# Two conditioned transformer layers on one core: the preparation put in another order, with most modulation blocks inside the slots of the first samples

## What is computed

```python
mod = swish(c) @ w_mod + b_mod
sh_msa, sc_msa, g_msa, sh_mlp, sc_mlp, g_mlp = split(mod, 6)
xn = _ln(x) * (1 + sc_msa) + sh_msa
q, k, v = heads(xn @ w_qkv + b_qkv)
q, k = _ln(q, g_q), _ln(k, g_k)          # layer 0 only
o = softmax(q @ k.T * HD ** -0.5) @ v
x = x + g_msa * (o @ w_proj + b_proj)
xn2 = _ln(x) * (1 + sc_mlp) + sh_mlp
x = x + g_mlp * (gelu(xn2 @ w1 + b1) @ w2 + b2)
```

## Time and profile before

| what | value |
|---|---|
| median of three runs | 2647.27 us (2644.73 to 2651.49) |
| the profiled execution | 2644.36 us, with a span of 2642.6 us |
| TensorE (PE) busy | 2495.9 us, 94% |
| VectorE (DVE), ScalarE (ACT), GpSimd (POOL) busy | 69%, 60%, 26% |
| mean granted clock of TensorE | 0.982 of full speed |
| first MLP product starts (slot 49 of sample 0) | 231.64 us |

### The profile page before, as it was taken

One profiled execution on the slowest core, in us unless ns is written; L12 is line 12 of the kernel. 1 busy time (PEld: TensorE's weight loads), 2 busy tenths in 40 slices (PEclk: granted clock), 3 DMA queues, 4 the chain that ended last, 5 costly groups with the idle time before them and its releaser, 6 DMA issues.

```text
span 2642.6 us, 59200 instructions
## 1 busy us (share of the span) xinstructions
PE 2495.9 (94%) x22440; PEld 2107.7 (80%) x22440; DVE 1831.6 (69%) x3700; ACT 1572.5 (60%) x2861; POOL 677.2 (26%) x937
## 2 busy tenths in 40 slices
PE   4678999999999999999999999999999999999998
PEld 2456888888888888888887788888888888888878
DVE  4466677677777777777776776776667776767764
ACT  2355666666666666666655656565556656565653
POOL 1112232232232232232322122222221222222122
PEclk8779999999999999999999999999999999999999
DMA  5654544534544544543644644554455445544531
GB/s 156 124 146 77 90 76 76 90 76 76 91 76 74 91 77 74 91 77 69 127 80 83 135 80 78 84 95 79 77 88 90 80 78 90 89 77 80 87 58 41
DMA packets 209849, 229.91 MB, mean 87 GB/s; under 512 B 20968, under 2 KB 197328, under 8 KB 209056
## 3 DMA queue, kind: packets, MB, share of 16 engines
q1 hardware_dynamic: 197124, 196.74, 44.6%
q10 hardware_dynamic: 12444, 29.39, 3.6%
HBM read 88.50 MB, written 28.12 MB: 44 GB/s over the span
## 4 chain that ended last, share of the span: by engine, by line
PE 63%; SPq 13%; DMA 10%; DVE 8%; issue 5%; ACT 1%; POOL 0%; DVEq 0%; POOLq 0%; ACTq 0%
PE psum L691 15%; DMA attn_k_stack<-attn_qk_hi 9%; SPq L1244 8%; PE psum L784 7%; PE psum L855 5%; PE psum_exp L760 5%; PE psum_exp L691 5%; PE psum_max L691 5%; PE psum L857 5%; PE psum L856 5%; SPq L1249 4%; PE psum_max L773 4%; DVE attn_maxima L1022 3%; PE psum L698 2%; PE psum L747 1%
## 5 line engine op out<-in xcount | busy, mean ns | idle before, releaser
L893 ACT ACTIVATE attn_probs<-psum_exp 128x1024 f32<-128x1024 f32 x512 | 524.6, 1025 | 429.7 <-PE psum_exp L760 426.9
L1022 DVE TENSOR_REDUCE attn_maxima<-psum_max 128x4 f32<-128x1024 f32 x512 | 622.3, 1215 | 130.5 <-PE psum_max L773 124.6
L1190 POOL TENSOR_TENSOR mlp_x<-mlp_x,mlp_gated 128x288 f32<-128x288 f32 x128 | 103.1, 806 | 1164.9 <-DVE mlp_gated L1039 1164.9
L855 PE MATMUL psum<-mlp_w_fc_hi,mlp_hidden_hi 128*128 128x288 f32 x1152 | 346.7, 301 | 17.8 <-DVE attn_o_split L1107 15.5
L691 PE MATMUL psum<-attn_ln_split,w_qkv_split 128*128 128x256 f32 (+3 forms) x2240 | 341.3, 295 | 7.5 <-DVE attn_ln_split L1126 7.2
L857 PE MATMUL psum<-mlp_w_fc_hi,mlp_hidden_lo 128*128 128x288 f32 x1152 | 340.1, 295 | 0.0
L856 PE MATMUL psum<-mlp_w_fc_lo,mlp_hidden_hi 128*128 128x288 f32 x1152 | 339.8, 295 | 0.0
L691 PEld LDWEIGHTS psum<-attn_ln_split,w_qkv_split 128*128 128x128 f32 (+3 forms) x2240 | 281.7, 181 | 58.4 <-issue 16.9
L784 PE MATMUL psum<-attn_probs,attn_v 128*20 128x256 f32 x4096 | 276.4, 388 | 1.1 <-ACT attn_probs L893 1.1
L760 PE MATMUL psum_exp<-attn_q_stack,attn_k_stack 64*128 64x256 f32 x2048 | 259.6, 332 | 14.1 <-DMA attn_q_stack<-attn_neg_max_lo 10.2
L773 PE MATMUL psum_max<-attn_k_stack,attn_q_stack 62*128 62x256 f32 x2048 | 214.7, 288 | 50.4 <-DMA attn_k_stack<-attn_qk_hi 40.7
(11 more groups left out here) (175 smaller groups left out, 4372.5 us busy)
## 6 DMA issues: line engine op xcount, KB each, us to landing
attn_q_stack<-attn_qk_hi SPq DMA_DIRECT2D x256, 128.0 KB
attn_k_stack<-attn_qk_hi SPq DMA_DIRECT2D x256, 128.0 KB
mlp_gate_and_gated_bias<-modulation ACTq DMA_DIRECT2D x64, 288.0 KB, 3.3
attn_q_stack<-attn_qk_lo SPq DMA_DIRECT2D x128, 128.0 KB
attn_k_stack<-attn_qk_lo SPq DMA_DIRECT2D x128, 128.0 KB
attn_x<-in_x_dram SPq DMA_DIRECT2D x32, 288.0 KB, 7.2
attn_gate<-modulation SPq DMA_DIRECT2D x64, 144.0 KB, 3.4
mlp_x<-in_x_dram SPq DMA_DIRECT2D x32, 288.0 KB, 3.7
```

What stands on the lines that cost most here:

```text
L855: q.matmul(bank[:, 0:C], h_hi[:, c, cols], w2_hi[:, c, :], start=(c == 0), stop=False)
L893: q.activation(probs[r][:], ps_exp[:], ACT.Exp, scale=SCORE_SCALE).then_inc(S["exps"], 1)
L1022: q.tensor_reduce(maxes[g % 2][:, p // QUARTER, :, p % QUARTER, :], ps_max[:].rearrange("p a (t n) -> p a t n", t=TT), AX.X, ALU.max).then ...
```

## The change

Nothing is computed otherwise; instructions and DMAs change place.

- SP's queue first loads the q, k, v weights, then two samples' x, then the output projection's weights. ScalarE's queue loads w_mod of layer 0 in two parts: first the columns of two blocks with the bias, then the other four.
- In front of the slots there are only the products, rows, transposes and copies of two blocks of layer 0. VectorE centres the weights between them. The spread matrices are copied at slot -36.
- The other four blocks of layer 0 are at slots -24 to -21, their transposes at -19. The load for layer 1 is issued by ScalarE at slot -18, its blocks are at -11 to -6 and their transposes at -4.
- arrange(0) goes to SP at slot -27 and arrange(1) to slot 43. Layer 0's MLP weights are loaded at slots 14 and 15 and split at 26, 27, 32 and 33. The output projection's split goes to -16 and -15.

The core of the diff:

```diff
-CENTRE_AT, QKV_HI_AT, QKV_LO_AT, PROJ_HI_AT, PROJ_LO_AT = -57, -54, -53, -20, -19
-MOD_AT, MOD_TR = range(-18, -12), -11
-W_AT, W1_SPLIT, W2_SPLIT = (-6, SPAN * (B - 1) + 51), (6, SPAN * (B - 1) + 58), (10, SPAN * (B - 1) + 64)
-W2_AT = (-5, SPAN * (B - 1) + 59)
+MOD_OUT_AT, QKV_HI_AT, QKV_LO_AT, SPREAD_OUT_AT, PROJ_HI_AT, PROJ_LO_AT = -56, (-57, -50), (-54, -49), -36, -16, -15
+MOD_AT, MOD_TR, MOD_LOAD = (-24, -23, -22, -21, -11, -10, -9, -8, -7, -6), (-19, -4), -18
+ARRANGE_AT = (-27, 43)
+W_AT, W1_SPLIT, W2_SPLIT = (14, SPAN * (B - 1) + 51), (26, SPAN * (B - 1) + 58), (32, SPAN * (B - 1) + 64)
+W2_AT = (15, SPAN * (B - 1) + 59)
...
-        def load_mod(q, l):
+        def load_mod(q, l, part):
             w, bias, b2 = MOD_NAMES[l]
-            q.dma_start(w_mod[:], a[w].rearrange("(i p) n -> p i n", p=K3)).then_inc(S["w_mod_loaded", l], 16)
-            q.dma_start(b_mod[:], a[bias].rearrange("(o n) -> o n", o=1).broadcast_to([B, 6 * C])).then_inc(S["w_mod_loaded", l], 16)
-            q.dma_start(b_2[:], a[b2].rearrange("(o n) -> o n", o=1).broadcast_to([B, C])).then_inc(S["w_mod_loaded", l], 16)
+            cols = (slice(0, 2 * C), slice(2 * C, 6 * C), slice(0, 6 * C))[part]
+            q.dma_start(w_mod[:, :, cols], a[w][:, cols].rearrange("(i p) n -> p i n", p=K3)).then_inc(S["w_mod_loaded", part], 16)
+            if part != 1:
+                q.dma_start(b_mod[:], a[bias].rearrange("(o n) -> o n", o=1).broadcast_to([B, 6 * C])).then_inc(S["w_mod_loaded", part], 16)
+            if part != 0:
+                q.dma_start(b_2[:], a[b2].rearrange("(o n) -> o n", o=1).broadcast_to([B, C])).then_inc(S["w_mod_loaded", part], 16)
+        def load_raw(q, which):
+            wq, bq, wp, bp = ATTN_NAMES[0]
+            w, bias, cols, at = ((wq, bq, slice(0, 3 * C), slice(0, 3 * C)), (wp, bp, slice(0, C), slice(3 * C, 4 * C)))[which]
+            for dst, src in raw_moves(raw0[:, :, at], w, bias, cols):
+                q.dma_start(dst, src).then_inc(S["raw_loaded", which], 16)
...
-            load_mod(q, 0)
+            load_raw(q, 0)
             for g in range(XA_RING):
                 load_xa(q, g)
+            load_raw(q, 1)
...
-            q.wait_ge(S["mod_mm"], 6)
-            q.wait_ge(S["mod_rows_ready"], 1)
-            load_mod(q, 1)
-            q.dma_start(mod_d[0], rows[0][:]).then_inc(S["mod_stored", 0], 16)
...
-            wq, bq, wp, bp = ATTN_NAMES[0]
-            for dst, src in raw_moves(raw0[:, :, 0:3 * C], wq, bq, slice(0, 3 * C)) + raw_moves(raw0[:, :, 3 * C:4 * C], wp, bp, slice(0, C)):
-                q.dma_start(dst, src).then_inc(S["raw_loaded"], 16)
             q.preload_act_table_set("natural_log_exp_and_others")
+            load_mod(q, 0, 0)
             q.wait_ge(S["cond_loaded"], 16)
             q.activation(silu_a[:], cond[:], ACT.Exp, scale=-1.0).then_inc(S["silu_exp"], 1)
+            load_mod(q, 0, 1)
+        def spread_out(q):
...
+        MOD_STEPS = [(0, j) for j in (1, 0, 2, 4, 3, 5)] + [(1, j) for j in (1, 0, 2, 4, 3, 5)]
+        MOD_PARTS = ((0, (0, 1)), (0, (2, 3)), (1, (0, 1, 2, 3)))
+        MOD_FIRST, MOD_TURN_BANK = (0, 2, 6, 12), (0, 0, 2)
...
+            if n >= 2:
+                q.wait_ge(S["mod_row"], n - 1)
+            if n == 2:
+                q.wait_ge(S["spread_ready"], NQK)
...
+            centre_means(q)
+            centre(q, 0)
+            mod_row(q, 0)
+            centre(q, 1)
+            mod_row(q, 1)
+            mod_rest(q, 0)
             q.memset(psum[PV_BANK][:, 0:N], 0.0).then_inc(S["pv_cleared"], 1)
-            mod_rest(q, 0)
-            mod_out(q, 0)
...
-                    mod_product(q, 1, T - MOD_AT.start)
-                if T == MOD_TR:
-                    mod_turn(q, 1)
+                    mod_product(q, 2 + MOD_AT.index(T))
+                if T in MOD_TR:
+                    mod_turn(q, 1 + MOD_TR.index(T))
...
+                if T == SPREAD_OUT_AT:
+                    spread_out(q)
+                if T == MOD_LOAD:
+                    q.wait_ge(S["mod_mm"], 6)
+                    q.wait_ge(S["mod_rows_ready"], 1)
+                    load_mod(q, 1, 2)
...
-                    mod_row(q, 1, T - MOD_AT.start)
-                if T == MOD_AT.stop:
-                    mod_rest(q, 1)
-                if T == MOD_TR + 1:
-                    mod_out(q, 1)
+                    mod_row(q, 2 + MOD_AT.index(T))
+                if T + 1 in MOD_TR:
+                    mod_rest(q, 1 + MOD_TR.index(T + 1))
+                if T - 1 in MOD_TR:
+                    mod_out(q, 1 + MOD_TR.index(T - 1))
...
-                if T == MOD_AT.stop + 1:
-                    q.wait_ge(S["mod_rows_ready"], 2)
-                    q.dma_start(mod_d[1], rows[1][:]).then_inc(S["mod_stored", 1], 16)
-                if T == 10:
+                if T in MOD_TR:
+                    l = MOD_TR.index(T)
+                    q.wait_ge(S["mod_rows_ready"], l + 1)
+                    q.dma_start(mod_d[l], rows[l][:]).then_inc(S["mod_stored", l], 16)
+                if T == ARRANGE_AT[0]:
+                    arrange(q, 0)
+                if T == ARRANGE_AT[1]:
                     arrange(q, 1)
-                if T == 0:
+                if T == 8:
```

More of the change, by code:

```diff
@@ L500, in mod_rest @@
[L500 to L509 removed]
+            if n in MOD_FIRST:
+                part = MOD_FIRST.index(n)
+                q.wait_ge(S["w_mod_loaded", part], (32, 32, 48)[part])
@@ L510, in mod_turn @@
+        def mod_turn(q, part):
+            l, kinds = MOD_PARTS[part]
+            bank = psum[MOD_TURN_BANK[part]]
+            q.wait_ge(S["mod_rest"], (2, 4, 8)[part])
+            if part == 1:
+                q.wait_ge(S["mod_t_ready"], 2)
+            for k in kinds:
+                at = MOD_KINDS[k]
                 for c in range(2):
@@ L996, in slots_dve @@
             for T in SLOTS:
-                if T == CENTRE_AT:
-                    centre(q)
-                if T == QKV_LO_AT:
+                if T == MOD_OUT_AT:
+                    mod_out(q, 0)
+                if T == QKV_LO_AT[0]:
                     split_qkv_lo(q)
+                if T == QKV_LO_AT[1]:
+                    split_qkv_last_lo(q)
+                if T == VALUE_AT[0][0]:
+                    for v in v_sb:
+                        q.memset(v[:, :, :, HD:HD + 1], 1.0)
+                        q.memset(v[:, :, :, HD + 1:VW], 0.0).then_inc(S["v_ones_placed"], 1)
                 if T == VAR_AT:
```

121 lines of the change are left out of this document (61 added, 60 removed).

## The result

The changed kernel takes 2651.08 us (median, 2648.78 to 2659.21) where the kernel before took 2646.69 (2643.58 to 2651.49) on the same chip: ratio 1.002, 95% interval 1.0011 to 1.0029, so 4.4 us slower. The interval leaves out 1, so the loss is real, but it is small: it stays inside the 0.3% that the prediction took as no change. The forecast was 2648. Its profiled execution has a span of 2649.3 us, 6.7 above that of before, and the first MLP product, where the full stretch begins, starts at 236.51 instead of 231.64.

What follows compares the result with a forecast made beforehand. TensorE, busy from 240 us on, was taken as the bound, so the front only moves that stretch's begin. Terms summed to +0.8 on the profiled 2644.36, giving 2645.2; the median lies 2.9 above, so 2648, range 2636 to 2661.

Steps and rivals of the forecast that it cites:

- What bounds the kernel: TensorE from 240 us on; a change in the front only moves that stretch's begin, and each microsecond arrives at the end.
- The start: Up to sample 0's first projection: weights land earlier, projection at 32.6 instead of 52.56; gain 19.9 us (17 to 22).
- Rival (4): Start not won: ACT's 864 KB land at 15 instead of 11.4, adding 3.6, 2652; counted within the forecast's 52%.
- Four blocks: Slots -24 to -21, between sample 0's variance and first spread product: products and DVE rows delay it; loss 5.2 (3 to 9).
- The load of layer 1: Modulation weights issued just ahead of sample 0's first stack DMA, sharing the DMA engines; loss 6 us (0 to 9).
- Six blocks: Slots -11 to -6, moved from sample 0's stack stretch into its score stretch; loss 8 us (6 to 13).
- The MLP load: At slots 14 and 15 it meets sample 2's stack stretch, loss 6 (0 to 8); leaving sample 1's stack stretch gains 1.1.
- The splits: MLP weight splits leave the second score stretch, so the maximum that releases SP comes earlier; gain 5.4 us (4 to 7).
- The first split behind: First MLP split returns at slots 26 and 27, in the third score stretch; loss 2 us (0 to 4.5).
- Rivals (1): The transfers hide: stack DMAs hold their pace beside a big load, the two losses of 6 fall; 2638, chance 22%.
- (2): Everything hides, the blocks too, and the start's gain arrives whole: -20, 2627; chance 5%.
- Rival (3): Blocks run cold at the lower clock: ten at 3.09 instead of 1.64 add 14.5, 2662; chance 18%.

Runs made afterwards that it cites:

- the fastest version: Changed kernel's front, blocks in idle places, MLP load at slots -9 and -8, MLP splits at 31, 32, 34, 35; 2621.26 us, 0.9905 of the kernel before.
- the experiment: Changed kernel, but ScalarE issues the second part of layer 0's modulation weights only when the q, k, v weights have landed; one run, 2653.84 us.
- the later version: Changed kernel's front, other transfers and blocks in idle places, MLP load at slots 14 and 15; 2630.03 us, ratio 0.9938 to the kernel before.

## Why the prediction was right, step by step

- **What bounds the kernel** held. The first MLP product moved by +4.9 and the median by +4.4; in the fastest version by -25.3 and -25.1. In the other versions the two differ by up to 3.2 us. The sign that the prediction named, this product within 3 us of its old time, was missed all the same.
- **The start** (-19.9, came -17.7). The mechanism held, two numbers did not. The q, k, v weights were counted to land near 9 us and landed at 15.30, because the bandwidth was divided by what is needed first and not by all that is queued; the experiment gives 2.8 us of it back. Rival (4) had the late landing on the wrong queue: the two blocks were done at 17.9, near the 17.4 counted, and set nothing.
- **Four blocks** (+5.2, came +5.0): right, and gone in the versions that put them elsewhere.
- **The load of layer 1** (+6, came +8.9, at the end of its range). The mechanism held and the term was mis-sized, by its arithmetic. The shares of the earlier trace rows, 67.1% of 13 us and 112.8% of 6 us, make 15.5 full us of work and not 13. (Counted by packets it is the same: 2,224, at the rate of the last 865 in 6 us, take 15.4.) That leaves 1.1 us of slack in the 16.6 and not 3.5, and a loss of 8.9, which is what came (7.7 to 8.9 over five traces). The estimate of 6.3 by packets took the rule of the Trainium skill, page "DMA: Bandwidth & Descriptors", section "Queues, rings and completion order", as one packet of the profile from each queue in turn. The trace does not agree with that: 288 packets went through beside 26, though from 10 to 12 us in the start the two queues moved 64 and 62. The page lets a packet hold some 9 to 17 descriptors, so the profile's packets need not be the page's; which of the two was wrong, the rule or the counting, no run here shows. A share by bytes, which gave 3, is further off still.
- **Six blocks** (+8, came +7.4): the size is right, its make-up only in part. In three other executions of the same code the stretch is 27.0 to 27.1 us, so +9.8 to +9.9, and the +7.4 near the +8 is in part luck. Without their products 2.4 to 4.9 us come back, not 7, as the clock then stays low. What cost the rest (rows, copies, the clock) was not taken apart further.
- **The MLP load** (+6, came +4.2; 4.8 at sample 1, 5.2 at sample 2 in the later version) and its going from sample 1 (-1.1, came -1.5): held.
- **The splits** (-5.4, came -4.5; -4.9 alone) held. **The first split behind** (+2, came +1.4) was right as a difference only by chance: in the fastest version its removal gives 4.0, within the 0 to 4.5 named.
- **Not foreseen**: +1.8 in sample 3's score stretch, by a lower clock on the same products, seen also with the splits alone moved; the cause stays open.
- Rivals (1) and (2) fell with sample 0's stretch of 27.6. Rival (3) fell as to the blocks, though not by as much as this trace says: the first took 2.46 us and the others 1.64, but in the other executions the first took 3.09 and the second 2.3 to 2.5, so that one and a half of the six were cold. It had asked for five cold blocks of ten.

The forecast of +0.8 stands against +4.9 at the first MLP product. The errors partly cancel: 2.2 in the start, 2.9 in the load, 1.8 in the clock and 0.9 in the splits, against 1.8 the other way at sample 2's stack and 1.8 in smaller ones. So the closeness of the total is in part luck: single terms were off by up to 2.9 us.

## What to carry to other kernels

Before a bulk load is moved, list every transfer on the path, small ones too, and find where the load is really issued (the time in the trace, not the slot): it needs a window as long as itself in which none of them is due. Work that leaves the front pays only if it lands in time in which its engine waits; here the 17.7 us won in front were all spent again, and with the same pieces in idle places 25 us arrived at the end. When work is taken off TensorE in a stretch full of waits, expect part of it back as a lower clock.

## What the runs showed of the hardware

- **A small DMA beside a bulk load.** Of the negated maxima, two DMAs of SP of 8 KB each, the second took 10.63 us to land beside a load of 2.9 MB, and TensorE waited 7.34 us for it. With the load elsewhere (slot -9) TensorE does not wait for them at all in that stretch. In the changed kernel itself it waited 6.18 us for them at 151.16, but inside sample 2's stack stretch, at whose end it waited another 8.37 us for the stack's own DMAs.
- **A bulk load shuts out another queue.** From 56 to 64 us the load's queue moved 288 packets at 99.3% and the stack's 26 at 1.6%, though its DMAs had been issued from 54.46 on.
- **VectorE held by GpSimd.** An operation of 0.30 us took 5.40 beside three clears of 1.80 each that followed one another: it did not get in between two of them, and the profile counts all of it as busy. That is not so of each operation: where the clears come later, the copies took 1.87 instead of 0.37 and ended with the first clear, about one clear's length, and the sum over heads took 2.07 either way. The Trainium skill, page "SBUF — State Buffer", section "Who interferes with whom", says that copy and tensor_scalar can take a port pair that GpSimd shares, that whoever is second is blocked for the other's whole instruction, and that tensor_reduce never contends; the trace agrees, and adds that the block can be several instructions long, as in the 5.40 us.
- **SP's issues stretch.** In sample 0's stack stretch of the changed kernel, beside the load, two issues took 3.77 us, where two took 1.26 a few microseconds earlier:

```profile
65.05 3.77 SPq L1293 DMA_DIRECT2D attn_k_stack<-attn_qk_hi  x2
```

- **Less work, lower clock.** 24 us of a stretch had a mean granted clock of 0.86 with the six blocks (0.78 in three other executions of them) and 0.50 without their products.
